# Row sums, the adding of x and bias, and one more base product moved to other places of a graph, mixer and feed-forward layer

## The chip, the cores and the metric

One core of a Trainium2 chip runs the whole layer. Its engines work side by side, each through a list of instructions of its own, and wait for one another by semaphores: TensorE (PE, matmuls), VectorE (DVE), ScalarE (ACT), GpSimd (POOL) and SyncE (SP, which issues most transfers). The metric is the device time of one execution in microseconds. A run of the profiler gives one execution's trace besides: every instruction with its start and duration, and what ended the idle time before it.

## The reference

`x` has 1250 rows of 1024 numbers; 40000 edges go from `src` to `dst`. After a layer norm three things are added: `x` itself, a graph attention over the edges, and a mixer without softmax. A feed-forward part in simulated 4-bit numbers follows.

```
xn = layernorm(x)
g  = rms(xn) @ W_down
xl, xr = g @ Wl, g @ Wr                     # 4 heads of 64
e = att . leaky_relu(xl[src] + xr[dst])     # self edges too
gnn = segment_softmax(e, dst) * xl[src], summed by dst, @ W_up
q, k, v = xn @ Wq.T + bq, xn @ Wk.T + bk, xn @ Wv.T + bv
mix = ((q @ k.T) * SCALE) @ v @ Wo.T + bo
x = x + gnn + mix
y = quantized(layernorm(x)) through gate, up, silu, down
out = x + y
```

## The kernel before

**The mixer in another order.** As nothing stands between its products, `mix` is written as `xn` times one 1024 x 1024 matrix plus one row. TensorE builds the matrix in groups of eight matmul pairs of 128 x 512 in float32 (a float32 matmul shows as two instructions): `gram` (16 groups, xn' xn), `p` (times Wv, 16), `kv` (Wk, 16), `t1` (Wo, 16), `t2` (Wq, 16). The row needs sums over the products: `sum_p0` adds, in 16 steps of VectorE over the slots `wslot`, the rows of Wv weighted by the column sums, and `p0c` (a tiny product between p 13 and p 14) turns the result; `sum_bias` adds in 8 steps the rows of t1's result weighted by bq, and `bias` (two matmuls) sums over partitions. Both start only when all their sums are there. Behind `bias` come the `base` groups, two for each block of 128 rows of xn, for the first EARLY = 7 of the C = 10 blocks; they wait for the taking of the last `t2`.

**Four banks, and takes.** Group n writes bank n % 4 of `acc` and waits until group n - 4 has been taken, that is copied out by VectorE (p, p0c, kv, bias; L1436 to L1448) or by ScalarE (t1 L1049, t2 L1056, base L1053).

**The rounds.** The attention runs over 62 rounds (0 to 61), each of 5 or 6 neighbours for one block of 128 nodes. GpSimd gathers the rows of round g + 3 (L559, one indirect transfer for each neighbour, four buffers) and in its middle rescales the running sum of round g (`rescale`, L679). VectorE adds the receiver (L1478), multiplies (L1632), reduces (L1634, L1639), and closes the round before with a sum (`close`, L1486). ScalarE takes exponentials (L1103) and multiplies (L1116), the second half of them after VectorE has closed the round before. A product's take stands ahead of its round, in the list of the engine that makes it.

**The order of the takes.** A small planner (`round_of`) walks through the groups: each adds 7 us (p0c 2, bias 1) to a clock that begins at PRODUCTS_AT, waits for group n - 4, and is rounded up to a round that is to begin at 196 + 8.1 g. The result fixes in which round each take stands. t2 15 falls in round 54, the bias takes too, the base takes in 56, 58, 59 and 61 and behind the last round. `sum_p0` stands in rounds 1 to 8, two in each, `sum_bias` in 46 to 53, one in each, both behind the closing of the round before.

**x and the base.** Once the bias product is done, SyncE loads x again into `base` (L516), behind the twelve transposing loads of the quantized weights (L510, L512), which wait for the last t2 product. GpSimd adds the bias row to a block of x (`add_bias`, L692) in rounds 56 to 61 and behind them, and the base product of the block (`add_base`, L700) after the rounds.

**Before the rounds** VectorE quantizes the three weights of the feed-forward part, in 12 pieces. SyncE stores each (`store(q)`), loads the second half of Wv into `view(4)` (2 MB, L494), then the rows bv and bk (L496, L497), without which no p group can be taken. TensorE computes between `hid` groups a product `tri` x `tot` that turns counts of receivers into offsets (L795).

**The tail.** Attention comes back through DRAM, is turned, and for every block and half an `x2` product adds gnn @ W_up (L916), and for blocks from EARLY on the mixer's eight matmul pairs too (L913). VectorE adds it to `base` with row sums (`residual`, L1589), then runs the quantization and the feed-forward part block by block. X2_PLAN gives for each (block, half) its bank, the step in which TensorE makes it and the step in which VectorE adds it.

## Time and profile before

| | us |
|---|---|
| median of 3 runs | 975.21 |
| lowest, highest | 972.39, 977.58 |
| the profiled execution | 969.87 |
| its span in the trace | 968.1 |
| PE busy | 861.4 (89%) |
| DVE busy | 841.0 (87%) |
| ACT busy | 555.2 (57%) |
| POOL busy | 508.8 (53%) |

The chain that ended last, followed back, lies to 53% on DVE, 13% on PE and 13% on ACT, with 15% of issue. The span is short of the run's time by 1.8 us at its ends. Busy shares are means over stages with different limits: the stage before the rounds (to about 194 us), the rounds (to 751), the base products behind them (to 776) and the tail. Instruction rows read: start, duration, engine, line, operation, output and inputs, and in brackets the idle time of that engine in front of it with what ended it.

### The profile page before, as it was taken

The numbers are of one execution on the slowest core, as the hardware profiler recorded it, in microseconds if no ns is written. First come the engines' busy times: TensorE is split into PE (matmuls) and PEld (weight loads), VectorE is DVE, ScalarE is ACT, GpSimd is POOL, SyncE is SP. The second block draws the span as 40 slices with busy tenths as digits, with TensorE's granted clock in tenths as the row PEclk, the third lists the DMA queues.
The fourth block names the chain that finished last, engine by engine and source line by source line (L and its number), as shares of the span: only waits on it lengthen the run. The fifth ranks groups of instructions, "written<-read, shape, count | busy, mean of one in ns | idle before, by whom it ended". The sixth has DMA issues, their size and how long they took to land.

```text
span 968.1 us, 9537 instructions
## 1 busy us (share of the span) xinstructions
PE 861.4 (89%) x2734; PEld 418.8 (43%) x2734; DVE 841.0 (87%) x971; ACT 555.2 (57%) x1949; POOL 508.8 (53%) x529
## 2 busy tenths in 40 slices
PE   4979999999949999999999899991999988989754
PEld 3865455644415444443443344440444443434321
DVE  7999989769999999999988899799886059999995
ACT  3303124237676887878879797887778042443332
POOL 5200363557667777677777677687786620010001
PEclk9989999999988999999999999996999999999968
DMA  9231724443543433554335533339721211123124
GB/s 295 89 126 13 215 56 159 137 164 89 85 163 117 150 91 94 176 179 116 95 101 171 175 95 101 87 89 232 291 71 40 71 43 44 48 61 61 27 43 82
DMA packets 64946, 109.97 MB, mean 114 GB/s; under 512 B 29223, under 2 KB 36036, under 8 KB 64874
## 3 DMA queue, kind: packets, MB, share of 16 engines
q0 software_dynamic: 19856, 55.42, 22.6%
q1 hardware_dynamic: 45034, 53.92, 17.0%
q8 instruction: 21, 0.34, 0.1%
q14 instruction: 35, 0.29, 0.1%
HBM read 89.15 MB, written 17.17 MB: 110 GB/s over the span
## 4 chain that ended last, share of the span: by engine, by line
DVE 53%; issue 15%; PE 13%; ACT 13%; DMA 3%; POOL 1%; another core or an unknown queue 1%; SPq 0%; DVEq 0%; POOLq 0%; ACTq 0%
PE acc L759 10%; ACT round_mem L1116 10%; DVE acc_sb L1486 7%; DVE z L1634 6%; DVE turned L1632 6%; DVE turned L1478 4%; DVE round_mem L1232 3%; DVE round_mem L1236 2%; DVE round_mem L1231 2%; DVE round_mem L1228 2%; DVE round_mem L1233 2%; ACT pz L1103 2%; DVE round_mem L1229 2%; DVE round_mem L1230 2%; DVE big_b L1440 1%
## 5 line engine op out<-in xcount | busy, mean ns | idle before, releaser
L559 POOL DMA_INDIRECT round_mem<-msg_table,idx x352 | 344.2, 978 | 134.2 <-issue 80.5
L1116 ACT ACTIVATE round_mem<-round_mem,pz 128x65 f32<-128x65 f32 x1408 | 358.0, 398 | 32.4 <-issue 14.0
L759 PE MATMUL acc<-wslot,big_a 128*128 128x512 f32 x512 | 225.4, 601 | 7.8 <-ACT big_b L1049 3.8
L759 PEld LDWEIGHTS acc<-wslot,big_a 128*128 128x128 f32 x512 | 97.8, 193 | 133.8 <-issue 123.9
L1486 DVE TENSOR_REDUCE acc_sb<-round_mem 128x260 f32<-128x1820 f32 (+1 forms) x62 | 121.6, 1962 | 33.7 <-ACT round_mem L1116 19.0
L759 PE MATMUL acc<-big_b,wslot 128*128 128x512 f32 x256 | 112.1, 600 | 5.1 <-remote 3.5
L1103 ACT ACTIVATE pz<-z 128x7 f32<-128x7 f32 (+1 forms) x248 | 56.5, 296 | 103.0 <-DVE z L1639 77.2
L759 PE MATMUL acc<-wslot,big_b 128*128 128x512 f32 x256 | 110.0, 592 | 0.0
L1478 DVE TENSOR_TENSOR turned<-round_mem,turned 128x1560 f32<-128x1560 f32 (+1 forms) x62 | 105.4, 1700 | 2.7 <-DMA round_mem<-msg_table,idx 0.4
L1634 DVE TENSOR_REDUCE z<-turned 128x24 f32<-128x1560 f32 (+1 forms) x62 | 105.1, 1695 | 2.1
L1632 DVE SCALAR_TENSOR_TENSOR turned<-turned,att_sb 128x1536 f32<-128x1536 f32 (+1 forms) x62 | 103.5, 1670 | 0.0
L759 PE MATMUL acc<-big_a,xhat_t 128*128 128x512 f32 x224 | 96.3, 592 | 0.0
L759 PE MATMUL acc<-big_b 128*128 128x512 f32 (+3 forms) x240 | 80.4, 494 | 0.0
L759 PEld LDWEIGHTS acc<-big_b,wslot 128*128 128x128 f32 x256 | 49.1, 192 | 68.2 <-issue 63.8
L759 PEld LDWEIGHTS acc<-wslot,big_b 128*128 128x128 f32 x256 | 48.6, 190 | 61.2 <-issue 61.0
L759 PEld LDWEIGHTS acc<-big_a,xhat_t 128*128 128x128 f32 x224 | 42.6, 190 | 53.9 <-issue 53.1
L679 POOL TENSOR_TENSOR round_mem<-acc_sb,pz 128x260 f32<-128x260 f32 x62 | 45.6, 736 | 23.9 <-DVE acc_sb L1486 16.8
L759 PEld LDWEIGHTS acc<-big_b 128*128 128x128 f32 x240 | 42.8, 193 | 35.2 <-issue 29.5
L726 POOL TENSOR_TENSOR rstd<-small,minus_half 128x1 f32<-128x1 f32 x10 | 7.0, 705 | 89.2 <-ACT small L1129 89.2
L732 POOL DMA_DIRECT2D out_x<-acc_sb x9 | 8.1, 895 | 72.2 <-ACT acc_sb L1139 68.5
L1182 ACT ACTIVATE round_mem<-acc,cscale 128x512 f32<-128x512 f32 x10 | 6.9, 688 | 62.4 <-PE acc L946 62.4
L1046 ACT COPY big_a<-acc 128x512 f32<-128x512 f32 x16 | 9.2, 587 | 57.8 <-PE acc L759 35.9
(222 smaller groups left out, 1060.2 us busy)
## 6 DMA issues: line engine op xcount, KB each, us to landing
big_b<-in_x SPq DMA_DIRECT2D x18, 512.0 KB, 6.0
round_mem<-msg_table,idx POOLq DMA_INDIRECT x352
out_x<-big_b SPq DMA_DIRECT2D x9, 512.0 KB, 2.7
out_x<-acc_sb POOLq DMA_DIRECT2D x9, 512.0 KB, 5.3
wslot<-in_wv_t SPq DMA_DIRECT2D x2, 2048.0 KB
wslot<-in_wk_t SPq DMA_DIRECT2D x2, 2048.0 KB
wslot<-in_wo_t SPq DMA_DIRECT2D x2, 2048.0 KB
wslot<-in_wq SPq DMA_DIRECT2D x2, 2048.0 KB
```

Source lines behind the costliest of these rows:

```text
L559: pool.indirect_dma_start(xg[g % 4][:, j, :], None, msg_table, bass.IndirectOffsetOnAxis(idx[:, c, j0 + j:j0 + j + 1], 0)).then_inc(xg_in[ ...
L679: nc.gpsimd.tensor_tensor(halves_of[g % 3][:, :, :, n].rearrange("p i (h d) -> p i h d", d=MR), running[c].rearrange("p (i h d) -> p i h d ...
L759: mm = nc.tensor.matmul(o(acc[:, n % 4, :]), a, b, start=first, stop=last)
L1103: ins = nc.scalar.activation(pz[:, g % 2, 0:slots + 1, h], z[:, g % 3, 0:slots + 1, h], ACT.Exp, scale=-1.0, bias=z[:, (g + 1) % 3, top_sl ...
L1116: ins = nc.scalar.activation(to[:, :, j], xg[g % 4][:, j, h * HR + 1:(h + 1) * HR], ACT.Copy, scale=pz[:, g % 2, j, h:h + 1])
L1228: step(nc.vector.tensor_tensor(blocks(v), blocks(v), spread(inv), ALU.mult))
L1229: step(nc.vector.tensor_scalar(t.bitcast(I32), v.bitcast(I32), EXPONENT, HALF_BIT, ALU.bitwise_and, ALU.bitwise_or))
L1232: step(nc.vector.scalar_tensor_tensor(to, v, 6.0 * UP + FP4_MAX, t, ALU.min, ALU.subtract))
L1478: return nc.vector.tensor_tensor(m4[:, 0:n], xg[g % 4][:, 0:n, :].rearrange("p j (h d) -> p j h d", d=HR)[:, :, :, 0:MR], receiver.unsquee ...
L1486: nc.vector.tensor_reduce(running[c].rearrange("p (i f) -> p i f", i=2), halves_of[g % 3][:, :, :, 0:n + 1], AX.X, ALU.add).then_inc(sum_d ...
L1632: step(nc.vector.scalar_tensor_tensor(m4[:, 0:slots, :, 1:MR], m4[:, 0:slots, :, 1:MR], 0.0, att_sb[0:NC].unsqueeze(1).to_broadcast([NC, s ...
L1634: step(nc.vector.tensor_reduce(zz[:, 0:slots, :], m4[:, 0:slots], AX.X, ALU.add))
```

## The change

- EARLY is 8: one more block gets its base product ahead of the tail, two groups more.
- PRODUCTS_AT is 173: the planner's clock starts 6 us earlier, by which most takes stand in the same round or one earlier. t2 15 and the bias takes now stand in round 53, the base takes in 55, 57, 59, 60 and behind the last round (eight there).
- Eight of the sixteen p0 sums stand before round 0 and eight in rounds 0 to 3. The bias sums stand in rounds 41 to 48.
- The rows bv and bk are loaded ahead of the last piece's store and of view(4).
- The product of the counts stands behind all hid groups instead of before the last two.
- VectorE adds x and bias in rounds 54 to 61, for blocks 0 to 7, and behind them block 8, then the bases of blocks 0 to 6, block 9's x, and the base of block 7. GpSimd does none of that any more.
- X2_PLAN has other banks and steps for most entries; one line of five stands below.

```diff
-EARLY = 7
+EARLY = 8
...
-PRODUCTS_AT, GROUP_STEP = 179.0, {"p0c": 2.0, "bias": 1.0}
+PRODUCTS_AT, GROUP_STEP = 173.0, {"p0c": 2.0, "bias": 1.0}
...
+BIAS_SUMS_AT, X_AT = 41, 54
 X2_PLAN = (
-    (0, 0, 6, (-2, 1), (-2, 0)), (0, 1, 2, (-2, 1), (-1, 0)), (1, 1, 0, (-2, 3), (-1, 0)), (1, 0, 3, (-2, 5), (-1, 0)),
+    (0, 1, 6, (-2, 1), (-2, 0)), (0, 0, 2, (-2, 1), (-2, 0)), (1, 1, 6, (-2, 3), (-2, 0)), (1, 0, 1, (-2, 5), (-1, 0)),
...
@@ SyncE @@
-            for q in range(8, 12):
+            for q in range(8, 11):
                 store(q)
-            sp.wait_ge(w_quantized, 3)
-            sp.dma_start(view(4), uses[4][1]).then_inc(w_in[0], 16)
             sp.wait_ge(acc_full, index_of["gram", 15] + 1)
             sp.dma_start(bv_bc, bv.rearrange("(a d) -> a d", a=1).to_broadcast([P, D])).then_inc(vb_in, 16)
             sp.dma_start(bk_bc, bk.rearrange("(a d) -> a d", a=1).to_broadcast([P, D])).then_inc(vb_in, 16)
+            store(11)
+            sp.wait_ge(w_quantized, 3)
+            sp.dma_start(view(4), uses[4][1]).then_inc(w_in[0], 16)
...
@@ GpSimd: add_bias and add_base go @@
-                if g > LAST - 6:
-                    add_bias(g - (LAST - 5))
             for g in range(LAST - 2, LAST + 1):
                 rescale(g)
-                add_bias(6 + g - (LAST - 2))
...
-            for c in range(EARLY):
-                add_base(c)
-            add_bias(C - 1)
...
@@ TensorE @@
-                if n == 4:
-                    pe.wait_ge(tot_done, 1)
-                    pe.wait_ge(pool_const, 10)
-                    nc.tensor.matmul(tp[0:DG_HI, 1, 0:1], tri, tot[:], start=True, stop=True).then_inc(off_done, 1)
...
+            pe.wait_ge(xt_taken, 2 * C)
+            pe.wait_ge(tot_done, 1)
+            pe.wait_ge(pool_const, 10)
+            nc.tensor.matmul(tp[0:DG_HI, 1, 0:1], tri, tot[:], start=True, stop=True).then_inc(off_done, 1)
...
@@ VectorE @@
             def residual(c, h):
-                dve.wait_ge(base_added, min(c + 1, EARLY))
-                if c == C - 1:
-                    dve.wait_ge(bias_added, C)
...
+            def add_bias(c):
+
+                n = rows(c)
+                dve.wait_ge(x_in[c], 32)
+                ins = nc.vector.tensor_tensor(base[0:n, c, :], x_last if c == C - 1 else base[:, c, :], bias_bc[0:n, :], ALU.add)
+                ins.then_inc(bias_added, 1)
+
+            def add_base(c):
+
+                dve.wait_ge(acc_taken["act"], taken[index_of["base", ORDER["base"].index((c, 1))]])
+                b = base[:, c, :].rearrange("p (k n) -> p k n", k=KB)
+                step(nc.vector.tensor_tensor(b, base_at[c], b, ALU.add))
...
+            for n in range(KB):
+                sum_p0(n)
             dve.wait_ge(xr_in, 16 * C)
...
-                if 1 <= g <= 8:
-                    sum_p0(2 * g - 2)
-                    sum_p0(2 * g - 1)
-                if 46 <= g < 46 + KB:
-                    sum_bias(g - 46)
+                if g < KB // 2:
+                    sum_p0(KB + 2 * g)
+                    sum_p0(KB + 2 * g + 1)
+                if BIAS_SUMS_AT <= g < BIAS_SUMS_AT + KB:
+                    sum_bias(g - BIAS_SUMS_AT)
+                if X_AT <= g < X_AT + C - 2:
+                    add_bias(g - X_AT)
             close(LAST)
             for n in due("dve", None):
                 take(n)
+            add_bias(C - 2)
+            dve.wait_ge(bias_added, C - 1)
+            for c in range(EARLY - 1):
+                add_base(c)
+            add_bias(C - 1)
+            dve.wait_ge(bias_added, C)
+            add_base(EARLY - 1)
```

VectorE where round 0 begins, before. L1476 and L1478 add the receiver of round 0, L1440 takes a p group (it needs `vb_in`, the rows bv and bk), L1632 begins the round:

```order
L1514 COMPARE_AND_BRANCH
L1498 UNCONDITIONAL_BRANCH
L1476 COPY turned<-xr_sb 128x260 [waits xr_in]
L1478 TENSOR_TENSOR turned<-round_mem,turned 128x1560 [waits xg_in0,dve_step]
L1440 SCALAR_TENSOR_TENSOR big_b<-big_b,colsum,acc 128x512 [waits vb_in,acc_full,dve_step]
L1440 SCALAR_TENSOR_TENSOR big_b<-big_b,colsum,acc 128x512 [waits vb_in,acc_full]
L1632 SCALAR_TENSOR_TENSOR turned<-turned,att_sb 128x24x64
L1634 TENSOR_REDUCE z<-turned 128x24 [waits dve_step]
L1638 COPY z<-top_first 128x4 [waits dve_step]
```

And changed; line numbers have moved (L1453 and L1455 are the old L1476 and L1478, L1417 the old L1440, L1623 the old L1632), L1581 and L1584 are p0 sums:

```order
L1491 COMPARE_AND_BRANCH
L1475 UNCONDITIONAL_BRANCH
L1581 TENSOR_SCALAR big_b<-wslot,colsum 128x512 [waits w_in1,colsum_done,acc_full]
L1584 SCALAR_TENSOR_TENSOR big_b<-wslot,colsum,big_b 128x512 [waits p0_summed] x7
L1453 COPY turned<-xr_sb 128x260 [waits xr_in]
L1455 TENSOR_TENSOR turned<-round_mem,turned 128x1560 [waits xg_in0,dve_step]
L1417 SCALAR_TENSOR_TENSOR big_b<-big_b,colsum,acc 128x512 [waits vb_in,acc_full,dve_step]
L1417 SCALAR_TENSOR_TENSOR big_b<-big_b,colsum,acc 128x512 [waits vb_in,acc_full] x2
L1623 SCALAR_TENSOR_TENSOR turned<-turned,att_sb 128x24x64
L1625 TENSOR_REDUCE z<-turned 128x24 [waits dve_step]
L1629 COPY z<-top_first 128x4 [waits dve_step]
L1630 TENSOR_REDUCE z<-z 128x4 [waits dve_step]
```

Eight sums now stand in front of the receiver's add, and three takes instead of two in front of round 0.

ScalarE around the take of the last t2 group, before. L1056 is a take of t2 into `big_a`; L1103 are exponentials, with `128x7` in a round of six neighbours (53) and `128x6` in one of five (52, 54); L1116 are the multiplications:

```order
L1056 ACTIVATE big_a<-acc 128x512 [waits acc_full]
L1103 ACTIVATE pz<-z 128x7 [waits z_done]
L1103 ACTIVATE pz<-z 128x7 x3
L1116 ACTIVATE round_mem<-round_mem,pz 128x65 [waits e_done]
L1116 ACTIVATE round_mem<-round_mem,pz 128x65 x11
L1116 ACTIVATE round_mem<-round_mem,pz 128x65 [waits sum_done]
L1116 ACTIVATE round_mem<-round_mem,pz 128x65 x11
L1056 ACTIVATE big_a<-acc 128x512 [waits acc_full]
```

And changed (L1033, L1080 and L1093 are the old L1056, L1103 and L1116):

```order
L1033 ACTIVATE big_a<-acc 128x512 [waits acc_full]
L1080 ACTIVATE pz<-z 128x6 [waits z_done]
L1080 ACTIVATE pz<-z 128x6 x3
L1093 ACTIVATE round_mem<-round_mem,pz 128x65 [waits e_done]
L1093 ACTIVATE round_mem<-round_mem,pz 128x65 x9
L1093 ACTIVATE round_mem<-round_mem,pz 128x65 [waits sum_done]
L1093 ACTIVATE round_mem<-round_mem,pz 128x65 x9
L1033 ACTIVATE big_a<-acc 128x512 [waits acc_full]
```

The second take, that of t2 15, stood between rounds 53 and 54 and stands between 52 and 53.

VectorE at the end of the rounds, before. L1486 closes a round, L1492 to L1494 finish the attention of a block, L1589 are residuals:

```order
L1486 TENSOR_REDUCE acc_sb<-round_mem 128x260 [waits rescaled,mul_done,dve_step]
L1632 SCALAR_TENSOR_TENSOR turned<-turned,att_sb 128x24x64 [waits e_done]
L1634 TENSOR_REDUCE z<-turned 128x24 [waits dve_step]
L1639 TENSOR_REDUCE z<-z 128x4 [waits dve_step]
L1486 TENSOR_REDUCE acc_sb<-round_mem 128x260 [waits rescaled,mul_done,z_done]
L1486 TENSOR_REDUCE acc_sb<-round_mem 128x260 [waits rescaled,mul_done]
L1492 TENSOR_SCALAR stats<-acc_sb 128x4 [waits sum_done]
L1493 RECIPROCAL stats<-stats 128x4 [waits dve_step]
L1494 TENSOR_TENSOR xr_sb<-acc_sb,stats 128x256 [waits dve_step]
L1589 SCALAR_TENSOR_TENSOR big_b,less_mean<-turned,big_b 128x512 [waits x2_full,base_added]
```

And changed (L1463 closes, L1591 adds x and bias, L1598 adds a base, L1563 is a residual):

```order
L1463 TENSOR_REDUCE acc_sb<-round_mem 128x260 [waits rescaled,mul_done,z_done]
L1591 TENSOR_TENSOR big_b<-big_b 128x1024 [waits x_in7]
L1463 TENSOR_REDUCE acc_sb<-round_mem 128x260 [waits rescaled,mul_done]
L1469 TENSOR_SCALAR stats<-acc_sb 128x4 [waits sum_done]
L1470 RECIPROCAL stats<-stats 128x4 [waits dve_step]
L1471 TENSOR_TENSOR xr_sb<-acc_sb,stats 128x256 [waits dve_step]
L1591 TENSOR_TENSOR big_b<-big_b 128x1024 [waits x_in8]
L1598 TENSOR_TENSOR big_b<-xhat_t,big_b 128x1024 [waits acc_taken_act,bias_added]
L1598 TENSOR_TENSOR big_b<-xhat_t,big_b 128x1024 [waits acc_taken_act,dve_step] x6
L1591 TENSOR_TENSOR big_b<-round_mem,big_b 98x1024 [waits x_in9,dve_step]
L1598 TENSOR_TENSOR big_b<-xhat_t,big_b 128x1024 [waits acc_taken_act,bias_added]
L1563 SCALAR_TENSOR_TENSOR big_b,mean_var<-turned,big_b 128x512 [waits x2_full,dve_step]
```

Behind the last close nine adds of 1024 columns and one of 98 rows stand ahead of the first residual, the last of them with a wait for ScalarE's last take.

## Rows read from the trace of the kernel before

**Rows 1.** Busy time by stage: window, then for each engine busy us (instructions), clock, DMA.

```profile
205.00:300.00 95.00, 81.57 (x194) 37.54 (x194) 92.92 (x82) 66.71 (x272) 62.36 (x65) 0.93 0.40 100
...
500.00:600.00 100.00, 94.51 (x215) 40.92 (x214) 88.08 (x72) 84.24 (x326) 72.99 (x81) 0.98 0.45 134
...
680.00:778.00 98.00, 96.85 (x230) 43.02 (x229) 59.03 (x49) 57.96 (x220) 68.38 (x53) 1.00 0.33 108
```

**Rows 2.** TensorE in order of time: start, duration, line, operation, [idle before it <- releaser].

```profile
67.56 0.26 PE L795 MATMUL turned<-tot,round_mem 40*40 40x1 f32 x2 [5.79 <-issue]
...
290.79 3.58 PE L759 MATMUL acc<-minus_half,big_b 128*128 128x1 f32 x16 [12.36 <-DVE big_b L1610]
...
450.41 22.54 PE L759 MATMUL acc<-wslot,big_a 128*128 128x512 f32 x48 [2.08 <-ACT big_b L1049]
...
543.07 98.07 PE L759 MATMUL acc<-big_b,wslot 128*128 128x512 f32 x224 [3.54 <-remote]
...
676.75 3.42 PE L759 MATMUL acc<-big_b,minus_half 128*128 128x512 f32 x4 [20.00 <-DVE big_b L1621]
680.00 96.30 PE L759 MATMUL acc<-big_a,xhat_t 128*128 128x512 f32 x224
```

**Rows 3.** VectorE in order of time.

```profile
203.33 1.41 DVE L1440 SCALAR_TENSOR_TENSOR big_b<-big_b,colsum,acc 128x512 f32<-128x512 f32 x2 [7.35 <-issue]
...
249.13 1.77 DVE L1610 SCALAR_TENSOR_TENSOR big_b<-wslot,colsum,big_b 128x512 f32<-128x512 f32 x2
...
610.25 1.78 DVE L1486 TENSOR_REDUCE acc_sb<-round_mem 128x260 f32<-128x1560 f32 x1 [5.62 <-ACT round_mem L1116]
...
621.44 1.28 DVE L1621 SCALAR_TENSOR_TENSOR big_b<-big_b,bq_col 128x1024 f32<-128x1024 f32 x1
...
751.20 0.42 DVE L1494 TENSOR_TENSOR xr_sb<-acc_sb,stats 128x256 f32<-128x256 f32 x1
779.95 0.69 DVE L1589 SCALAR_TENSOR_TENSOR big_b<-turned,big_b 128x512 f32<-128x512 f32 x1 [28.33 <-POOL big_b L700]
...
790.71 1.23 DVE L1228 TENSOR_TENSOR round_mem<-round_mem 128x1024 f32<-128x1024 f32 x1
```

**Rows 4.** VectorE's waits from 779 to 968: us in total, times, longest.

```profile
DVE big_b L1589 <- PE acc L916: 3.9, 3, 1.5
DVE big_b L1594 <- PE turned L968: 3.1, 1, 3.1
```

**Rows 5.** ScalarE in order of time.

```profile
600.15 2.51 ACT L1116 ACTIVATE round_mem<-round_mem,pz 128x65 f32<-128x65 f32 x9 [3.96 <-remote]
...
642.10 1.06 ACT L1056 ACTIVATE big_a<-acc 128x512 f32<-128x512 f32 x2
...
667.96 0.58 ACT L1056 ACTIVATE big_a<-acc 128x512 f32<-128x512 f32 x1
...
678.87 0.58 ACT L1056 ACTIVATE big_a<-acc 128x512 f32<-128x512 f32 x1
```

**Rows 6.** SyncE in order of time, issues of transfers.

```profile
187.76 0.69 SPq L496 DMA_DIRECT2D big_b<-in_bv  x1
...
662.86 11.52 SPq L512 DMA_TRANSPOSE wslot<-gu_dram  x8
```

**Rows 7.** TensorE in windows of 1 us: busy us, granted clock, DMA share, GB/s.

```profile
677.00:678.00 1.00, 1.00 (x2) 0.50 1.00 365
679.00:680.00 1.00, 1.00 (x2) 0.66 0.87 340
```

**Rows 8.** GpSimd in order of time.

```profile
238.66 1.11 POOL L679 TENSOR_TENSOR round_mem<-acc_sb,pz 128x260 f32<-128x260 f32 x1 [1.27 <-DVE acc_sb L1486]
...
642.47 0.68 POOL L679 TENSOR_TENSOR round_mem<-acc_sb,pz 128x260 f32<-128x260 f32 x1
...
675.59 1.63 POOL L679 TENSOR_TENSOR round_mem<-acc_sb,pz 128x260 f32<-128x260 f32 x1 [1.36 <-DVE acc_sb L1486]
...
684.80 2.37 POOL L692 TENSOR_TENSOR big_b<-big_b 128x1024 f32<-128x1024 f32 x1 [3.94 <-DMA big_b<-in_x]
```

More of the change, by code:

```diff
@@ L529, in _ @@
             sp.wait_ge(added[1], 16 * 4)
-        round_of, freed, at = {}, {}, PRODUCTS_AT
-        for n in range(index_of["p", 0], len(groups)):
-            kind, i, _ = groups[n]
-            at = max(at, freed.get(n - 4, 0))
-            at += GROUP_STEP.get(kind, 7.0)
-            round_of[n] = max(0, math.ceil((at - ROUND_0_AT) / ROUND_STEP))
-            if kind == "base" and ORDER["base"][i][1] == 1:
-                round_of[index_of["base", ORDER["base"].index((ORDER["base"][i][0], 0))]] = round_of[n]
-            freed[n] = max(at, ROUND_0_AT + round_of[n] * ROUND_STEP) + 1.5
         @block.gpsimd
@@ L682, in rescale @@
                                         ALU.mult).then_inc(rescaled, 1)
-            def add_bias(c):
-                n = rows(c)
-                pool.wait_ge(x_in[c], 32)
-                if c == 0:
-                    pool.wait_ge(acc_taken["dve"], count["dve"])
-                if c == C - 1:
-                    pool.wait_ge(bias_added, c)
-                nc.gpsimd.tensor_tensor(base[0:n, c, :], x_last if c == C - 1 else base[:, c, :], bias_bc[0:n, :],
-                                        ALU.add).then_inc(bias_added, 1)
-            def add_base(c):
-                pool.wait_ge(bias_added, c + 1)
-                pool.wait_ge(acc_taken["act"], taken[index_of["base", ORDER["base"].index((c, 1))]])
-                b = base[:, c, :].rearrange("p (k n) -> p k n", k=KB)
-                nc.gpsimd.tensor_tensor(b, base_at[c], b, ALU.add).then_inc(base_added, 1)
-            assert round_of[index_of["bias", 1]] <= LAST - 5
             for g in range(1, LAST + 1):
@@ L986, in _ @@
                     x2(*i)
+        round_of, freed, at = {}, {}, PRODUCTS_AT
+        for n in range(index_of["p", 0], len(groups)):
+            kind, i, _ = groups[n]
+            at = max(at, freed.get(n - 4, 0))
+            at += GROUP_STEP.get(kind, 7.0)
+            round_of[n] = max(0, math.ceil((at - ROUND_0_AT) / ROUND_STEP))
+            if kind == "base" and ORDER["base"][i][1] == 1:
+                round_of[index_of["base", ORDER["base"].index((ORDER["base"][i][0], 0))]] = round_of[n]
+            freed[n] = max(at, ROUND_0_AT + round_of[n] * ROUND_STEP) + 1.5
         def due(engine, g):
@@ L1611, in sum_p0 @@
                 ins.then_inc(p0_summed, 1)
+            def add_bias(c):
[7 more added lines that the diff above has]
+                step(nc.vector.tensor_tensor(b, base_at[c], b, ALU.add))
+            assert round_of[index_of["bias", 1]] < X_AT <= LAST - (C - 3)
             def sum_bias(k):
```

3 lines of the change are left out of this document (1 added, 2 removed), and 8 rows, old and new, of the table X2_PLAN.

## The prediction

> **What bounds the kernel now.** First the busy time of each engine by stage [rows 1]. In the rounds (205 to 750) VectorE, ScalarE and GpSimd hand work to one another: up to 300 VectorE is busy 92.92 of 95 us; from 500 on it has 88.08 of 100, while GpSimd's 72.99 lie in 81 instructions that mostly have 0.3 us of issue between them, so it is nearly full. From 680 to 778 TensorE alone is full, 96.85 of 98.
>
> Second, TensorE's rows in order of time [rows 2]. It waits 20.00 us for the last row sum of the bias, does the bias product at 676.75, and from 680.00 the fourteen base groups without a gap: 96.30 us, 6.88 each. The first x2 products follow, and at 779.95 VectorE begins the first residual [rows 3]. The last attention was written at 751.20, so the rounds are not the limit here: **the base products set when the tail begins.** Behind 779.95 VectorE waits 3.9 us in three places for TensorE and 3.1 us before its last instruction [rows 4]; the tail is VectorE's own work, 968.1 - 779.95 = 188.15 us.
>
> So two things count: when the first base group starts, and how long the groups take. Its code waits until ScalarE has taken t2 group 15, which is written ahead of round 54: 678.87 + 0.58 [rows 5], and base began at 680.00.
>
> **The change, part by part.** The sum is made in the profiled execution: span 968.1, time 969.87, so 1.8 outside the span. The median of the runs shown is 975.21, 5.3 above; I carry the difference over to it.
>
> *a. The take moves one round.* By the new table t2 15 is taken ahead of round 53. That place in before is the take at 667.96 [rows 5]: 678.87 - 667.96 = **10.9 earlier**. The bias sums now end with round 48, so the 20.00 us wait goes; what is late next is this take, not TensorE. Group t2 15 may start when t2 11 is taken, ahead of round 50 (642.10 in before [rows 5], about 5 less by b and c), and ends near 645; the take comes near 660.
>
> *b. The p0 sums and the loads of bv and bk.* Before round 0 VectorE stands still for 7.35 us [rows 3], with p group 0 long done: bv was issued at 187.76 [rows 6], right behind 2 MB for wslot, and landed by 203.33, 15.6 later. Now it is issued about 181, behind the store of piece 10, with nothing large ahead; even after 15.6 it is there at 197. Eight sums fill the gap: two take 1.77 [rows 3], eight at most 7.1. The work on VectorE is the same in all, only its gap is gone, and up to 300 it is the bound: **7.35 earlier** once the rounds with sums are past. Bounds: 0 if something else is late, 7.35 in full. Its neighbours can follow: in 205 to 300 GpSimd is busy 62.36 of 95 us in 65 instructions, and later it has moved along.
> The p0c product then need not wait 12.36 us [rows 2], worth 0 by itself: already in before TensorE runs into takes later on (2.08 at 450.41, for ScalarE). So too the 5.79 in front of the counts' product at 67.56, now behind the last hid groups: TensorE comes earlier to p, while VectorE's chain to round 0 reads that product a whole piece of quantization later and stays.
>
> *c. The bias sums in rounds 41 to 48.* Ahead of the take stood six of them, now all eight, at 1.28 each [rows 3]: +2.6. VectorE can fill idle time with them: of its 11.9 idle us in 500 to 600 the larger part is spread thin, some 0.5 a round, which over rounds 41 to 46 is about 3. I take **0**, with +2.6 and -2.6 as bounds.
>
> *d. One more base.* Two groups of 6.88: **+13.75**, wholly on the path. In return two x2 products of the tail lose their eight long matmul pairs, 13.8 us of TensorE; but VectorE waits for it only 3.9 us there, at products that are short anyway. I take 0, at best -3.9. The new order of x2 products: 0 too; the nearest rows for a wait that it might bring are those three, 1.3 each.
>
> *e. The clock.* After the 20 us wait the granted clock was 0.50 (1.2 GHz), in the slice from 679 still 0.66 [rows 7], and the bias product bore it; base ran at 2.4 GHz. Now the bias product is done by about 650, base follows after a wait of some 10 us, and the slow 3.3 us fall on base groups: half of it, **+1.65** (0 to 1.8; the 224 matmuls from 543.07, also after a wait, took 98.07 instead of 96.30 [rows 2]).
>
> *f. x + bias, and the bases, on VectorE.* GpSimd's add took 2.37, the first after 3.94 of waiting for x [rows 8]; six leave the queue of its gathers. VectorE pays 1.23 (same shape, two tensors [rows 3]), eight times in rounds 54 to 61: at most +9.8 there. Base groups end near 771, attention would be ready by 751.6 - 7 + 10 = 755: cover of 15 us, so 0. The nine adds before the last one (11) lie in the same gap. The last waits for the take of base 15, two copies of 0.58 behind TensorE, and ends 2.4 behind it; the first x2 result comes 3.65 behind (779.95 - 776.30): 0, with 1 us to spare. In SP's queue the loads of x wait behind the twelve transposes, issued until 674.4 in before [rows 6] and about 11 earlier now; that is some 10 us before the first add wants a row, and if one is late the same cover holds. Taken off GpSimd, these adds gain nothing on the path either.
>
> **Sum**: -10.9 - 7.35 + 13.75 + 1.65 = **-2.85**; span 965.25, such a run 967.0, median **972.4**. All bounds on one side give -2.85 + 7.35 + 2.6 = +7.1 or -2.85 - 2.6 - 3.9 - 1.65 = -11.0; they will hardly meet. Own range 967 to 977.5.
>
> **Rivals.** *1. Faster: an interruption of ScalarE meets room.* In rounds 34 and 46 its small instructions stand up to 4 us apart with no wait of the program behind them (3.96 at 600.15 [rows 5]), the round takes 15 us instead of 8, and VectorE loses 5.62 in the one at 610.25 [rows 3]. If that one falls elsewhere, or where VectorE has sums to do, 5.6 is saved: -8.45, **966.8**. Against it: ScalarE's stream is nearly the same, so I expect it at the same place.
>
> *2. Slower: rounds 41 to 53 belong to GpSimd.* It has hardly room from 500 on [rows 1]. Then VectorE with sums and GpSimd are both full: +2.6 of c stays, nothing is absorbed, and rounds 49 to 52 give back less than 1.28 each, as gathers set their pace: +1.5 to +2.5. And rescale, 0.68 at 642.47, took 1.11 and 1.63 beside a sum on VectorE [rows 8]: 0.4 to 0.95 more in each of eight rounds, say 4 together. That is +8 to +9 and gives -2.85 + 8.4 = +5.5, **980.8**. It decides once base starts after 680.0 - 15.4 = 664.6, where two groups and the clock cost more than was gained.
> The Trainium skill (GPSIMD Engine Reference, 8. Key points) says that GpSimd shares its SBUF interfaces with VectorE and contends with instructions there that read two SBUF inputs. By that rule it comes to this rival; the rows agree in part, for it is 1.11 and 1.63 beside sums and 0.68 elsewhere.
>
> *3. The change doesn't do what it says:* bv and bk land late all the same, and the sums come on top: -2.85 + 6.6 = +3.7, **979.0**. Against it: their issue has only stores ahead. The same price stands for t2 15 being finished after its take is due, of which it has some 14 us in hand.
>
> **How the numbers follow.** Chances: forecast 0.52, rival 1 0.22, rival 2 0.18, rival 3 0.08. A measurement of this kernel can tell about 0.5% (4.9 us) from no change. The forecast spreads some 3 us each way, so 0.12 of its 0.52 lies beyond -4.9 and 0.40 within. Faster: 0.12 + 0.22 = 0.34. Same: 0.40 + 0.07 of rival 3 = 0.47. Slower: 0.18 + 0.01 = 0.19. The range, 965.5 to 979.5, takes in the forecast's own, rival 3 and most of rival 1, and leaves out rival 2.
>
> **What would show it.** Right: the takes of round 0 begin near 203 with no wait before them; TensorE's 20.00 and 12.36 are gone, and a wait of about 10 us ends with ScalarE's take of t2 15 near 660; sixteen base groups take 110 us plus 1.7, with a granted clock of 0.50 in the first 3; the first residual comes near 777, and 188 us follow; an add of x takes 1.23 and delays nothing. Wrong: base starting before 655 or after 665 (terms a to c), a gap among the base groups (a take too late), a first residual that waits for VectorE's own adds, or a tail that differs from 188 by over 2.

## The result and the profile after

The changed kernel takes 971.45 us (median of 19 runs, 967.86 to 974.49), the kernel before 975.15 (19 runs, 970.15 to 979.09). The ratio is 0.9957, 95% interval [0.9942, 0.9972]: a gain of 3.7 us, clear of noise in this comparison, and less than the 0.5% below which the prediction speaks of no change. The profiled execution has a span of 967.1 against 968.1 (time 969.57 against 969.87).

TensorE in order of time (start, duration, line, operation, [idle before it <- releaser]); the third row stands for sixteen base groups:

```profile
270.89 1.84 PE L726 MATMUL acc<-minus_half,big_b 128*128 128x1 f32 x16
...
647.95 3.41 PE L726 MATMUL acc<-big_b,minus_half 128*128 128x512 f32 x4 [4.53 <-ACT big_a L1033]
661.69 111.94 PE L726 MATMUL acc<-big_a,xhat_t 128*128 128x512 f32 x256 [10.34 <-issue]
```

The answering rows of before [rows 2] have waits of 12.36 and 20.00; both are gone. Base starts at 661.69 instead of 680.00 and runs without a gap for 111.94 instead of 96.30. The one take that base waits for, in ScalarE's order (t2 15, ahead of round 53; before at 678.87 [rows 5]):

```profile
656.25 4.96 ACT L1093 ACTIVATE round_mem<-round_mem,pz 128x65 f32<-128x65 f32 x20
661.06 0.58 ACT L1033 ACTIVATE big_a<-acc 128x512 f32<-128x512 f32 x1
```

VectorE where round 0 begins, and from the last attention to the first residual:

```profile
192.91 0.64 DVE L1581 TENSOR_SCALAR big_b<-wslot,colsum 128x512 f32<-128x512 f32 x1 [6.17 <-issue]
193.58 5.48 DVE L1584 SCALAR_TENSOR_TENSOR big_b<-wslot,colsum,big_b 128x512 f32<-128x512 f32 x7
...
201.26 2.06 DVE L1417 SCALAR_TENSOR_TENSOR big_b<-big_b,colsum,acc 128x512 f32<-128x512 f32 x3
203.24 1.76 DVE L1623 SCALAR_TENSOR_TENSOR turned<-turned,att_sb 128x1536 f32<-128x1536 f32 x1
...
741.45 1.22 DVE L1591 TENSOR_TENSOR big_b<-big_b 128x1024 f32<-128x1024 f32 x1
742.70 7.52 DVE L1598 TENSOR_TENSOR big_b<-xhat_t,big_b 128x1024 f32<-128x1024 f32 x6
761.17 1.23 DVE L1598 TENSOR_TENSOR big_b<-xhat_t,big_b 128x1024 f32<-128x1024 f32 x1 [10.95 <-ACT xhat_t L1030]
762.43 1.22 DVE L1591 TENSOR_TENSOR big_b<-round_mem,big_b 98x1024 f32<-98x1024 f32 x1
774.90 1.23 DVE L1598 TENSOR_TENSOR big_b<-xhat_t,big_b 128x1024 f32<-128x1024 f32 x1 [11.25 <-ACT xhat_t L1030]
777.29 0.69 DVE L1563 SCALAR_TENSOR_TENSOR big_b<-turned,big_b 128x512 f32<-128x512 f32 x1 [1.16 <-PE turned L883]
```

The takes of round 0 come with no wait, where [rows 3] had 7.35. The last add is done 1.16 before TensorE's first x2 result, so TensorE still sets the start of the tail, by a hair. From there the tail takes 967.1 - 777.29 = 189.81, against 188.15. VectorE's waits in it (us in total, times, longest; the first residual's own 1.16 is in the third row; before: [rows 4]):

```profile
DVE big_b L1598 <- ACT xhat_t L1030: 11.2, 1, 11.2
DVE big_b L1568 <- PE turned L935: 3.1, 1, 3.1
DVE big_b L1563 <- PE turned L883: 2.6, 2, 1.5
DVE big_b L1563 <- PE acc L883: 2.4, 2, 1.5
DVE round_mem L1534 <- ACT round_mem L1159: 0.7, 1, 0.7
DVE round_mem L1213 <- ACT round_mem L987: 0.6, 1, 0.6
```

So between the two profiled executions: base 18.31 earlier, two more groups and a low clock 15.64 longer, the tail 1.66 longer, in all -1.0. The medians differ by 3.7, because the profiled execution of before was 5.3 below its own median and that of after 1.9.

TensorE's granted clock where base starts (window of 1 us: busy us, clock, DMA share, GB/s):

```profile
661.00:662.00 1.00, 0.31 (x1) 0.31 (x2) 0.97 (x2) 0.64 (x2) 0.98 (x1) 0.50 1.27 327
664.00:665.00 1.00, 1.00 (x2) 0.34 (x1) 0.97 (x2) 0.97 (x4) 0.69 (x2) 0.50 1.21 320
665.00:666.00 1.00, 1.00 (x3) 0.43 (x2) 1.00 (x1) 1.00 (x6) 0.75 (x1) 0.81 1.28 189
```

It is 0.50 (1.2 GHz) after the wait, 0.81 in the slice from 665 and 1.00 (2.4 GHz) from 666 on; the sixteen groups take 111.94 instead of 16 x 6.88 = 110.1.

### The profile page after: what moved, and what is told of

The parts are those of the page before. It is cut to its first block, busy times and chain, and to the rows that moved or that the text cites. A ratio compares the mean times of both kernels' runs of the same rounds, so it can differ in the third digit from the quotient of the medians.

```text
span 967.1 us, 9516 instructions
## 1 busy us (share of the span) xinstructions
PE 869.2 (90%) x2725; PEld 420.3 (43%) x2734; DVE 859.7 (89%) x989; ACT 559.5 (58%) x1951; POOL 471.5 (49%) x512
## 4 chain that ended last, share of the span: by engine, by line
DVE 37%; PE 35%; ACT 17%; issue 9%; POOL 1%; another core or an unknown queue 0%; ACTq 0%; DVEq 0%; POOLq 0%
PE acc L726 29%; ACT round_mem L1093 13%; DVE z L1625 6%; DVE turned L1623 5%; DVE acc_sb L1463 5%; DVE turned L1455 4%; ACT pz L1080 2%; DVE round_mem L1208 2%; DVE round_mem L1209 2%; DVE round_mem L1213 2%; DVE round_mem L1205 1%; PE turned L935 1%; DVE round_mem L1210 1%; DVE big_b L1417 1%; PE acc L913 1%
## 5 line engine op out<-in xcount | busy, mean ns | idle before, releaser
L1093 ACT ACTIVATE round_mem<-round_mem,pz 128x65 f32<-128x65 f32 x1408 | 361.7, 399 | 38.0 <-issue 24.6
L726 PE MATMUL acc<-wslot,big_a 128*128 128x512 f32 x512 | 228.3, 607 | 11.9 <-remote 4.4
L1463 DVE TENSOR_REDUCE acc_sb<-round_mem 128x260 f32<-128x1820 f32 (+1 forms) x62 | 121.6, 1961 | 28.7 <-ACT round_mem L1093 16.4
L726 PE MATMUL acc<-big_a,xhat_t 128*128 128x512 f32 x256 | 111.9, 600 | 10.3 <-issue 10.3
L1455 DVE TENSOR_TENSOR turned<-round_mem,turned 128x1560 f32<-128x1560 f32 (+1 forms) x62 | 105.4, 1700 | 2.1
L1080 ACT ACTIVATE pz<-z 128x7 f32<-128x7 f32 (+1 forms) x248 | 56.3, 296 | 87.7 <-DVE z L1630 68.7
L1623 DVE SCALAR_TENSOR_TENSOR turned<-turned,att_sb 128x1536 f32<-128x1536 f32 (+1 forms) x62 | 103.6, 1671 | 0.0
L726 PEld LDWEIGHTS acc<-big_a,xhat_t 128*128 128x128 f32 x256 | 49.3, 193 | 73.8 <-issue 73.8
L935 PE MATMUL turned<-wslot,round_mem 128*128 128x512 bf16 x76 | 26.3, 506 | 21.4 <-ACT round_mem L1151 21.3
```

The lines of the kernel that those rows point to most:

```text
L726: mm = nc.tensor.matmul(o(acc[:, n % 4, :]), a, b, start=first, stop=last)
L935: mm = nc.tensor.matmul(tp[0:NC, h, :], h_t[c % 2][:, k, 0:NC], wdn_sb[:, k, h * HALF:(h + 1) * HALF], start=(k == 0), stop=(k == 3))
L1080: ins = nc.scalar.activation(pz[:, g % 2, 0:slots + 1, h], z[:, g % 3, 0:slots + 1, h], ACT.Exp, scale=-1.0, bias=z[:, (g + 1) % 3, top_sl ...
L1093: ins = nc.scalar.activation(to[:, :, j], xg[g % 4][:, j, h * HR + 1:(h + 1) * HR], ACT.Copy, scale=pz[:, g % 2, j, h:h + 1])
L1455: return nc.vector.tensor_tensor(m4[:, 0:n], xg[g % 4][:, 0:n, :].rearrange("p j (h d) -> p j h d", d=HR)[:, :, :, 0:MR], receiver.unsquee ...
L1463: nc.vector.tensor_reduce(running[c].rearrange("p (i f) -> p i f", i=2), halves_of[g % 3][:, :, :, 0:n + 1], AX.X, ALU.add).then_inc(sum_d ...
```

## The experiments

All kernels of one series ran on the same chip beside the kernel before. Each series had a chip of its own, and its own time, so that chip and time can't be told apart: before takes 953.3 us in the first (e1 to e4), 971.7 in the second (e5 to e8) and 953.8 in the third (e9 to e12). Ratios are to before on the same chip. From the traces: start of VectorE's round 0, start of base, first residual, the tail from there, span.

| kernel | round 0 | base | residual | tail | span | ratio [95%] |
|---|---|---|---|---|---|---|
| before | 204.65 | 680.00 | 779.95 | 188.15 | 968.1 | 1 |
| changed | 203.24 | 661.69 | 777.29 | 189.8 | 967.1 | 0.9957 [0.9942, 0.9972] |
| e1 | 202.38 | 641.59 | 744.41 | 200.6 | 945.0 | 0.9938 [0.9919, 0.9956] |
| e2 | 204.34 | 643.73 | 736.52 | 208.6 | 945.1 | 0.9924 [0.9902, 0.9945] |
| e3 | 202.44 | 652.45 | 768.90 | 189.9 | 958.8 | 1.0074 [1.0057, 1.0092] |
| e4 | 204.14 | 653.37 | 754.48 | 188.1 | 942.6 | 0.9918 [0.9899, 0.9936] |
| e5 | 203.00 | 660.85 | 776.76 | 189.8 | 966.6 | 0.9985 [0.9964, 1.0005] |
| e6 | 205.47 | 678.98 | 779.13 | 188.9 | 968.0 | 0.9990 [0.9969, 1.0012] |
| e7 | 202.46 | 660.80 | 762.45 | 189.9 | 952.4 | 0.9815 [0.9793, 0.9837] |
| e8 | 203.46 | 661.34 | 778.01 | 191.3 | 969.3 | 0.9986 [0.9967, 1.0005] |
| e9 | 201.98 | 651.23 | 752.43 | 188.5 | 940.9 | 0.9921 [0.9894, 0.9948] |
| e10 | 201.66 | 650.97 | 753.64 | 190.1 | 943.7 | 0.9914 [0.9888, 0.9940] |
| e11 | 202.98 | 643.64 | 755.77 | 190.2 | 946.0 | 0.9922 [0.9896, 0.9947] |
| e12 | 202.93 | 636.07 | 737.70 | 189.9 | 927.6 | 0.9747 [0.9719, 0.9775] |

**How many bases (e1, e2).** The changed kernel with

```diff
-EARLY = 8
+EARLY = 7
```

> The changed kernel with seven bases ahead instead of eight (EARLY = 7), all else as changed, its order of x2 products too. Theory: the eighth base is two groups of 6.88 us on TensorE, wholly on the path that sets the start of the tail, and gives back little there. Then the base groups start at 661.7 as in the changed kernel, end 13.8 earlier, near 760, the first residual comes near 763.5 instead of 777.3, the tail takes 188 to 193, and the span is about 953 (13 to 14 below the changed kernel's 967.1), the ratio to the kernel before about 0.982. Rival 1: the tail needs the eighth base, because TensorE has to do block 7's eight long matmul pairs twice there; then the tail takes about 190 + 13.8 = 203 and the span stays at 967. Rival 2: VectorE's adds at 741 to 751 and the wait for the attention become what starts the tail; they end by 752 in the changed kernel, ahead of 760, so this should not show.

and with `EARLY = 6`:

> The changed kernel with six bases ahead (EARLY = 6), all else as changed. Theory: the base groups end near 746, behind the last attention (741.5) and about when VectorE's adds (741.5 to 751) are done, so the first residual comes near 751 to 753; TensorE had 138 us busy in 190 of the tail with eight bases and would have 166 with six, in a tail whose first 60 us it was already filling to nine tenths, so the tail grows from 190 to some 195 to 204: span 946 to 957, between 7 faster and 4 slower than with seven. Rival 1: the tail is VectorE's alone, whatever TensorE has: tail 190, span 942. Rival 2: TensorE becomes the bound of the first half of the tail and gives all back: tail 203 or more, span 956 or more.

Both come out at nearly the same time, and their ratios are near the changed kernel's: the first residual of e1 comes 102.82 behind base's start, against 115.60 (777.29 - 661.69) in the changed kernel, so 12.8 sooner, but the tail takes 200.6, 10.8 longer. Rival 1 of e1 holds for this kernel. In e2 the first residual comes 7.9 sooner than in e1 (the base groups end at 727.88 and no longer set it), and the tail takes 8.0 longer, 208.6 where 195 to 204 was expected: rival 2 of e2. VectorE's waits in the tail of e1:

```profile
DVE big_b L1563 <- PE acc L883: 7.4, 3, 5.0
DVE round_mem L1213 <- ACT round_mem L987: 5.6, 1, 5.6
DVE big_b L1568 <- PE turned L935: 5.1, 1, 5.1
DVE big_b L1563 <- PE turned L883: 2.6, 2, 1.5
```

Against the changed kernel's rows above, 5.0 + 5.0 + 2.0 = 12 us more, for TensorE and for ScalarE behind it: about what was gained ahead of the tail. But e4, which also has seven bases and before's order of x2 products, has a tail of 188.1. So the order, not the number, was to be tried next.

**The order of the x2 products (e7, e8).** e7 is e1 with before's X2_PLAN, e8 the changed kernel (eight bases) with it:

```diff
 X2_PLAN = (
-    (0, 1, 6, (-2, 1), (-2, 0)), (0, 0, 2, (-2, 1), (-2, 0)), (1, 1, 6, (-2, 3), (-2, 0)), (1, 0, 1, (-2, 5), (-1, 0)),
+    (0, 0, 6, (-2, 1), (-2, 0)), (0, 1, 2, (-2, 1), (-1, 0)), (1, 1, 0, (-2, 3), (-1, 0)), (1, 0, 3, (-2, 5), (-1, 0)),
...
```

> The changed kernel with seven bases ahead and the kernel before's order of x2 products. With seven bases and the new order (e1) the first residual came 13.8 earlier, but VectorE then waited 5.6, 5.0 and 2.0 us more for block 7's long products, and the tail took 200.6. Theory: the new order is made for eight bases; with the old one the tail is 188 again, as with seven bases in the kernel before and in e4, and the ratio to the kernel before is 0.981 (12 us below e1's 0.9938). Rival: the tail's growth came with VectorE's adds or with the earlier start, not with the order; then the ratio stays at 0.993.

> The changed kernel with eight bases and the kernel before's order of x2 products. Theory (term d): VectorE waits for TensorE in the tail with the old order no more than with the new one, so the tail is 185 to 190 and the time that of the changed kernel within 2 us; the eighth base gives nothing back. Rival: the old order with eight bases has block 7's products short and saves the 3.9 us of waits: up to 4 below the changed kernel. Rival 2: the new order is what makes eight bases bearable, and this is slower by over 3.

e7 gives 0.9815 (95% interval 0.9793 to 0.9837) where 0.981 was expected: 953.88 us against 969.55 for the changed kernel (e5) on the same chip. Its tail is 189.9, as long as the changed kernel's, and its fourteen groups take

```profile
660.80 98.00 PE L726 MATMUL acc<-big_a,xhat_t 128*128 128x512 f32 x224 [15.23 <-issue]
```

e8 equals the changed kernel within a fraction of a us. Between e8 and e7 only the number of bases differs: medians 969.82 against 953.88, spans 969.3 against 952.4, 16.9 us, of which 15.56 lie ahead of the first residual. The sixteen groups of e8 take 113.02, the fourteen of e7 98.00: 13.75 of the difference are the two groups, the rest goes with the granted clock, which stays at 0.50 to 667 in e8 and to 664 in e7. **The eighth base costs all of its TensorE time and gives nothing back**, and the new order of x2 products is worth nothing either with eight bases (e5 and e8); with seven it is a loss (e1).

**The take of t2 15 (e3).** The changed kernel with one take put back:

```diff
             freed[n] = max(at, ROUND_0_AT + round_of[n] * ROUND_STEP) + 1.5
+        round_of[index_of["t2", 15]] += 1
```

> The changed kernel with ScalarE's take of t2 group 15 ahead of round 54 as in the kernel before, and not of round 53; all else as changed. Theory (term a): the base groups start when this take is done, so they start one round later, at the place where ScalarE in the changed kernel has done round 53's multiplications, about 671.6 + 0.6 instead of 661.7: 10.5 later, the first residual near 787.5, the span 977 to 978, the ratio to the changed kernel about 1.011. Rival: TensorE or VectorE's sums decided when base starts, and the take's place is worth nothing: span 967.

Base starts at 652.45, where e1 on the same chip, with the same program up to there, has 641.59: 10.9 later. The theory holds to half a us. The changed kernel itself did not run on this chip; by way of before, the ratio to it is 1.0074 / 0.9957 = 1.0117, or 1.0089 with the 0.9985 that e5 gives below.

**The p0 sums and the loads alone (e4).** The kernel before with these parts of the diff (SyncE's piece, the eight sums ahead of `add_receiver(0)`, eight in rounds 0 to 3).

> The kernel before with one part of the change alone: eight sums of p0 ahead of round 0 and eight in rounds 0 to 3, bv and bk loaded ahead of the last piece's store and of the second half of Wv. Takes, bias sums, bases and GpSimd's adds as before. Theory (term b): VectorE's 7.35 us of waiting before round 0 are filled with sums that stood in rounds 1 to 8, so round 9 begins about 8 earlier (near 283 instead of 291.3), the take of t2 15 and the base groups' start follow (672 instead of 680) and the span is 960 to 961, ratio to the kernel before about 0.992. Rival 1: something else holds the middle rounds (GpSimd's gathers, ScalarE's interruptions) and the gain is lost on the way: base start 677 to 680, ratio 0.997 to 1. Rival 2: the 20 us wait for the last bias sum, done in round 53, sets base's start: it moves with the rounds too, so the time is as in the theory.

Measured 0.9918, the gain of 8 that was expected. Its base starts at once behind the bias product:

```profile
649.79 3.78 PE L760 MATMUL acc<-big_b,minus_half 128*128 128x512 f32 x4 [14.26 <-DVE big_b L1622]
653.37 41.93 PE L760 MATMUL acc<-big_a,xhat_t 128*128 128x512 f32 x96
```

The wait is for VectorE's last bias sum. The take of t2 15 had been done by then (651.91 + 0.58). This small part of the change, alone, gives more than the whole (0.9957 in the first comparison, 0.9985 in e5, both on other chips; on this one e3 less the 10.9 us of its take gives 0.996).

**Two gates, one by one and together (e9, e10, e11).** e4 with `round_of[index_of["t2", 15]] -= 1` (e9), with

```diff
-                if 46 <= g < 46 + KB:
-                    sum_bias(g - 46)
+                if 41 <= g < 41 + KB:
+                    sum_bias(g - 41)
```

(e10), and with both (e11).

> e4 (the kernel before with the p0 sums and the loads of bv and bk moved) and ScalarE's take of t2 15 ahead of round 53 instead of 54; the bias sums still in rounds 46 to 53. Theory: the take and the last bias sum are two gates of the base groups, each closing near the same time; the take alone gives nothing, because TensorE then waits for the sum of round 53. Base starts where it does in e4 (on a chip with interruptions near 671), less 0 to 1, span as e4's; ratio to the kernel before 0.990 to 0.995. Rival: the take was the only gate, and this gives all of the 10.9: ratio 0.981 to 0.984.

> e4 and the bias sums in rounds 41 to 48 instead of 46 to 53; the take of t2 15 ahead of round 54. Theory: the take is now the gate; base starts 0.5 to 1 behind it, so 0 to 3 below e4: the bias product, 3.4 us, is out of the way, the sums cost VectorE nothing that shows. Ratio 0.988 to 0.995. Rival 1: the sums' place was the gate: 0.981 to 0.984. Rival 2: sums earlier cost the rounds more than they give where they leave: ratio over 0.995.

> e4 with both, the take ahead of round 53 and the bias sums in rounds 41 to 48; x, bias and bases still added by GpSimd, seven bases, the order of x2 products of before. Theory: with both gates moved base starts near 661 on a chip with interruptions, as in e7, and the span is e7's 952.4 within 1.5; the ratio is 0.9815, 10 us below e9 and e10, and the adds on VectorE (in e7) or on GpSimd (here) make no difference. Rival 1: the adds on VectorE carried part of e7's gain (six adds less among GpSimd's gathers): this is then 2 to 5 us slower than e7. Rival 2: they cost, and this is faster by the last add's 1.2 to 2.

Neither alone moves anything. This chip is another than e4's, of the same speed. Base starts 2.14 (e9) and 2.40 (e10) earlier than in e4, but round 0 had already begun 2.16 and 2.48 earlier in these executions, before any edit matters: net 0.0 and +0.1. Together base's start moves by 9.73, 8.6 of it beyond round 0's 1.16. And yet e11 is no faster, 0.9922 where 0.9815 was expected, and further behind e7 than its rival 1 allowed: the gain went into a third gate. In order of time in e11, TensorE, then GpSimd, then VectorE:

```profile
643.64 29.92 PE L761 MATMUL acc<-big_a,xhat_t 128*128 128x512 f32 x64 [6.17 <-ACT big_a L1058]
679.03 15.56 PE L761 MATMUL acc<-big_a,xhat_t 128*128 128x512 f32 x32 [5.47 <-ACT xhat_t L1055]
696.92 55.20 PE L761 MATMUL acc<-big_a,xhat_t 128*128 128x512 f32 x128 [2.33 <-ACT xhat_t L1055]
```

```profile
665.67 2.33 POOL L694 TENSOR_TENSOR big_b<-big_b 128x1024 f32<-128x1024 f32 x1 [12.35 <-DMA big_b<-in_x]
```

```profile
673.70 1.78 DVE L1488 TENSOR_REDUCE acc_sb<-round_mem 128x260 f32<-128x1560 f32 x1 [11.64 <-POOL round_mem L681]
```

GpSimd's first add of x, in round 56, waits 12.35 us for the row of x. The loads of x stand in SyncE's queue behind twelve transposes, issued until 657.5. While it waits, GpSimd gathers and rescales nothing, and VectorE stands for 11.64. ScalarE's first take of a base, ahead of round 56, is held up until 678.40, and TensorE, with four groups in its four banks, stops for 5.47 and again for 2.33. In before the same wait was 3.94 [rows 8] and in e6 3.35: there the loads of x were issued last, behind the bias product (680.20 in before), 5.8 us after the last transpose. In e4, e9 and e10 the bias product is done first, the transposes come last, and the wait is 9.42, 9.48 and 9.29. That e11 waits 3 us more is not for earlier rounds (its round 54 begins at 649.34, that of e10 at 648.08): the eight transposes of gu_dram took 15.54 us to issue in e11 and 11.44 in e10, and why stays open. The wait alone does not stop TensorE either: VectorE stands for 8.66 in e10, whose base groups began 7.3 later than e11's and run on without a gap. It takes both, such a round and takes of the bases that stand behind it. In the changed kernel and in e7 VectorE's add of x waits for nothing that shows, in e1 2.78 and in e12 3.73, and gathers go on beside it. e7 also takes the bases one round earlier than e11, so how much of the difference each of the two makes is not separated.

**The takes one round earlier again (e12).** e7 with

```diff
             freed[n] = max(at, ROUND_0_AT + round_of[n] * ROUND_STEP) + 1.5
+        for n in [index_of["t2", 15]] + [index_of["base", i] for i in range(2 * EARLY)]:
+            round_of[n] -= 1
```

> e7 (seven bases, old order of x2 products, the rest as changed) with the takes of t2 15 and of all bases one round earlier: t2 15 ahead of round 52. In e7 TensorE had done t2 15 at 642 and waited 15.2 us for the take. Theory: base starts behind the take's new place, 654.0 + 1.1, so near 655.3 instead of 660.8; the base groups end near 753.5, VectorE's adds (done by 751 or 752) stay ahead of that, the first residual comes at 757 and the tail takes 190: span 947, ratio to the kernel before 0.975 to 0.977. Rival 1: the last attention and VectorE's nine adds behind it now start the tail: gain only 2 to 4, ratio 0.978 to 0.980. Rival 2: ScalarE has to wait for t2 15 or for a base group there and holds up a round: no gain or a loss.

TensorE's base groups in e12, then VectorE's last add and first residual:

```profile
636.07 97.98 PE L726 MATMUL acc<-big_a,xhat_t 128*128 128x512 f32 x224 [6.25 <-ACT big_a L1035]
```

```profile
735.32 1.23 DVE L1600 TENSOR_TENSOR big_b<-xhat_t,big_b 128x1024 f32<-128x1024 f32 x1 [1.16 <-ACT xhat_t L1032]
737.70 0.69 DVE L1565 SCALAR_TENSOR_TENSOR big_b<-turned,big_b 128x512 f32<-128x512 f32 x1 [1.16 <-PE turned L883]
```

0.9747, slightly better than expected: 929.79 us where before takes 953.83. Base starts 5.5 earlier than in e1, the base groups have no gap, and VectorE waits only 1.16 us for the last take, so its adds are next to set the start of the tail. This version beats both kernels, and e7 does by less.

**The two kernels again (e5, e6).**

> The changed kernel, unaltered, on the chip of this series. In the first series e1, e3 and e4 ran on a chip on which the rounds ended some 20 us earlier and ScalarE's unexplained idle time (remote, issue) between the small instructions of a round was absent. Theory: the change is worth as much where ScalarE is never interrupted: ratio 0.993 to 0.997 to the kernel before; on such a chip round 9 begins 8 to 9 earlier than in the kernel before and the lead is kept evenly up to round 53, with no loss and return of 6 us as between rounds 38 and 47 of the first pair of traces. Rival: part of what the first pair showed came from interruptions that fell otherwise in the two runs; then the ratio here differs from 0.9957 by more than 0.003.

> The kernel before, unaltered, for a trace on the same chip as the others of this series. Theory: ratio 1.000; base starts 0.5 to 1 behind ScalarE's take of t2 15 ahead of round 54, with a wait of TensorE for the last bias sum of 14 to 20 us; ScalarE's idle time by remote and issue is small in its rounds if it is in those of the changed kernel, since it belongs to the chip or the run and not to the program. Rival: it belongs to the program (where its code lies), and this trace shows a round of 14 us at round 46 as the first did.

On this chip the change is worth 0.9985, with an interval that takes in no change: less than the expected 0.993 to 0.997, and the intervals of the two comparisons do just overlap. Base moves from 678.98 to 660.85, 18.13 us, as in the first pair (18.31); the span by 1.4. ScalarE's multiplications have 34.5 us of idle time before them in e5 and 34.0 in e6 (32.4 in before), so this was no chip without interruptions, for which e5's expectation was written. The round of 14 us that the kernel before had at round 46 takes 8.5 in e6, the same program, and others are long instead (10.5 at 33, 10.6 at 39). So such an interruption has no fixed place in the program. ScalarE's multiplications on the page of the changed kernel, and of e1 on the other chip (busy, mean ns | idle before them, and what ended most):

```profile
L1093 ACT ACTIVATE round_mem<-round_mem,pz 128x65 f32<-128x65 f32 x1408 | 361.7, 399 | 38.0 <-issue 24.6
```

```profile
L1093 ACT ACTIVATE round_mem<-round_mem,pz 128x65 f32<-128x65 f32 x1408 | 354.4, 398 | 7.0 <-DVE acc_sb L1463 3.0
```

The same instructions in the same order; 38.0 us of idle time here, 7.0 there. In e1 base starts 20 us earlier than in the changed kernel. The difference goes with the chip (or with the time of the series), not with the program, and the 20 us are over five times the 3.7 that the change was worth.

## Why the prediction was right, step by step

*What bounds the kernel.* Right: the base products set the start of the tail, and the tail is VectorE's. In the changed kernel their start hangs on ScalarE's take of t2 15; e3, which moves that take alone, moves the end. In before the take (done 679.45) was not the last gate: base began at 680.00, with the end of the bias product, 0.55 later.

*a, the take: -10.9.* Right in size (e3: 10.9 back). e9 and e11 show what else it needs: the bias sums moved, which the prediction names, and the bases' takes early enough to follow, which it does not price.

*b, p0 sums and loads: -7.35.* Right in kind. Round 9 begins at 283.21 instead of 291.31, 8.1 earlier, and e4 alone gives 0.8%. bv was issued at 180.17 and was there when wanted. The sums do not stand in the gap itself but ahead of the receiver's add, from 192.91, after a wait of 6.17 that before has too (6.41, ahead of the receiver's copy). It is as good, since the receiver's add moves behind the sums. The bound "7.35 in full" was too tight by some 0.7: round 0 begins 1.41 earlier, with one more take ahead of it, and eight sums less in the rounds are at most 8 x 0.88 = 7.1 (0.88 from [rows 3]), so at most 8.5; 8.1 came. The product of the counts, moved too, was not tried alone.

*c, bias sums: 0.* Right for base's start (e10: 0.1). On VectorE it is no zero: from round 41 to 49 e10 takes 69.95 against e4's 64.50, so five more sums cost 5.45, nearly their full 1.28 each; from 49 to 54 it takes 39.74 instead of 49.15, which gives back the sums and 3.19 us of VectorE's waits for the bias product. In the first pair of traces the same is seen: the lead shrinks from 8.6 at round 40 to 2.6 at round 46 and is 8.7 again at round 52. So the zero is the difference of two larger numbers, not 3 us of idle time filled up.

a to c together: 18.31 against 18.25. In the rows of ScalarE it splits otherwise: 10.91 for the place (678.87 - 667.96), 6.90 for all that lies ahead of the take (667.96 - 661.06, a lead of 8.1 at round 9 shrunk by then), and 0.50 for the bias product that base no longer waits for.

*d, one more base: +13.75.* Right: e7 against e8, with 1.3 more for the clock. The return in the tail was taken at 0, and there is none (191.3 against 189.9). What the prediction did not see is how far the order of the x2 products and the number of bases belong together (e1).

*e, the clock: +1.65.* Measured 111.94 - 110.1 = 1.9.

*f, adds on VectorE: 0.* In the sum right: the last add ended 1.16 before it was needed, where "1 to spare" stood. But the sentence that GpSimd's relief gains nothing on the path is in doubt. In e11, where GpSimd adds, its wait of 12.35 for x held up gathers, and TensorE lost 7.8 us. The prediction took the 3.94 of [rows 8] for the size of that wait; it is 9.3 to 12.4 once the bias product is done before the transposes are out. Whether the adds on VectorE are what lets a and c come through, or the earlier takes of the bases, no run separates. What the adds on VectorE cost GpSimd stands under rival 2.

*The tail: 188.15 kept.* It became 189.81; also 189.8 in e5. With eight bases and the old order it is 191.3, so the order of products is not the cause; 1.3 of it are two short waits of VectorE for ScalarE (0.7, 0.6) that before did not have. Why they come stays open. e7, e10, e11 and e12 have a tail as long (189.9 to 190.2) by another wait: VectorE waits 5.0 to 5.1 for TensorE ahead of its last instruction instead of 3.1 or 3.2 (before, e4, e9), and the granted clock in the stretch from 20 to 8 us before the end is 0.72 there and 1.00 in before, e4 and e9. e11 and e9 ran on one chip and differ in the place of the bias sums alone, far ahead of the tail; one execution of each was traced. The 1.66 are most of the difference between the sum (-2.85) and the spans (-1.0).

*The rivals.* Rival 1, a gain from an interruption that falls elsewhere, did not come, though its condition did: round 46, which took 14.07 in before, took 10.18, and round 34 took 10.12 instead of 11.78 (the prediction had read 15 for both). Other rounds were long instead (22, 25, 31 and 37: 10.1 to 10.7), and the lead at round 52 is 8.7, no more than the 8.4 it had been at round 10. The reason that the prediction gave against this rival, that the interruption keeps its place, is refuted by e6; that the losses came out even is luck. Rival 2: the busy time of VectorE and GpSimd was as high as feared, but rescale in rounds 41 to 53 took 0.67 to 0.69 throughout, never 1.11 or 1.63. In the rounds behind them it is different. Where a rescale begins 0.2 us after VectorE's add of x (1.22 us) has begun, it takes 1.57 or 1.58, in five rounds from 694 to 734; GpSimd, then VectorE:

```profile
694.45 1.58 POOL L671 TENSOR_TENSOR round_mem<-acc_sb,pz 128x260 f32<-128x260 f32 x1 [0.30 <-DVE acc_sb L1463]
```

```profile
694.29 1.22 DVE L1591 TENSOR_TENSOR big_b<-big_b 128x1024 f32<-128x1024 f32 x1
```

That is 0.9 more each time, 4.5 us of GpSimd, while the base groups ran without a gap, so it cost nothing here; the prediction did not count it under f. In e1 to e3 and e10 to e12 one rescale beside a bias sum takes 1.64 or 1.65. GpSimd's gathers show it too: those at 194.85, 196.25 and 197.82 are issued in 1.09, 1.27 and 1.27 instead of 0.95 beside the p0 sums, and so in every trace with eight sums ahead of round 0, e4 included, and not in before and e6. The rule of the Trainium skill (GPSIMD Engine Reference, 8. Key points), that GpSimd contends with instructions of VectorE that have two inputs in SBUF, agrees with these rows. So rival 2 had the price of one collision right, and its eight rounds escaped it in this execution. Rival 3 did not come: bv and bk were in time.

The time, 971.45 against 972.4, is nearer than the terms deserve. The sum gave 967.0 for a profiled execution, which took 969.57, 2.6 more; the 5.3 carried over from before was only 1.9, 3.4 less; and the two errors cancel by luck.

## What to carry to other kernels

Work that is put ahead of a phase to shorten it has to be priced in both: here an eighth base moved 13.8 us onto the path and took nothing off a tail that another engine fills, and without it the change is worth 1.8% (e7). A start that hangs on one wait often has a second and a third gate a few us behind: undo and apply the parts one by one and together, and look at what the freed time runs into. An order made by hand for one count of items is no order for another; when a count changes back, try the old order with it.
